# Cross attention and a two-expert feed-forward: an all-lane maximum at the start of GpSimd, expert chunks at step 10 in the shared tiles, column sums on GpSimd

## What is computed

```python
x = x + attention(layernorm(x), ctx, masks, Wq, Wk, Wv, Wo, bo)   # 16 heads of 64, 64 keys
z = layernorm(x)
top1 = argmax(softmax(z @ gate_w.T))                  # one of 2 experts
masked = z[None] * one_hot(top1).T[:, :, None]        # the expert that a row did not pick sees zeros
h = relu(einsum(masked, w1) + b1[:, None, :])
routing = (einsum(h, w2) + b2[:, None, :]).sum(axis=0)
shared = relu(z @ sw1 + sb1) @ sw2 + sb2
out = x + routing + shared
```

## Time and profile before

| what | value |
|---|---|
| median of 3 runs | 1909.89 us (1908.08 to 1910.09) |
| profiled execution, its own time | 1911.59 us |
| its span | 1909.8 us |
| TensorE busy | 1837.1 us, 96% |
| VectorE / ScalarE / GpSimd busy | 811.1 / 822.2 / 471.2 us |
| granted TensorE clock, mean | 0.984 |

### The profile page before, as it was taken

How to read it: one execution, slowest core, us unless ns; L and a number is a source line. 1 busy time by engine, 2 the same in 40 slices (tenths; PEclk the granted TensorE clock), 3 DMA queues, 4 the chain that set the end, 5 groups by cost and what they waited for, 6 DMA issues and landing times. The chain is left out here.

```text
span 1909.8 us, 33594 instructions
## 1 busy us (share of the span) xinstructions
PE 1837.1 (96%) x11584; PEld 1159.2 (61%) x11585; DVE 811.1 (42%) x1733; ACT 822.2 (43%) x1441; POOL 471.2 (25%) x443
## 2 busy tenths in 40 slices
PE   7979999999799999999999999999999999999997
PEld 5334445444456666666666666666666666666664
DVE  4977777777353444434333333222222222222222
ACT  3645555555333333334444444333333333433333
POOL 1036777777200000001000001121221112122111
PEclk9989999999899999999999999999999999999998
DMA  8225555555932232334433583822121111212100
GB/s 322 81 57 141 162 169 173 157 162 156 290 113 78 78 96 81 92 95 132 132 121 122 159 302 111 254 56 56 46 66 45 38 44 46 60 44 60 51 23 15
DMA packets 220647, 214.38 MB, mean 112 GB/s; under 512 B 121360, under 2 KB 162832, under 8 KB 220176
## 3 DMA queue, kind: packets, MB, share of 16 engines
q1 hardware_dynamic: 212640, 188.05, 33.1%
q0 software_dynamic: 7920, 25.17, 4.2%
HBM read 129.56 MB, written 58.98 MB: 99 GB/s over the span
## 5 line engine op out<-in xcount | busy, mean ns | idle before, releaser
L993 PE MATMUL pH<-room_a,room_w 128*128 128x256 f16 (+1 forms) x6336 | 768.9, 272 | 8.8 <-PEq L337 7.7
L1005 PE MATMUL pY<-room_w,room_a 128*128 128x512 f16 (+1 forms) x3120 | 755.3, 380 | 4.6 <-DVE room_a L1024 4.6
L993 PEld LDWEIGHTS pH<-room_a,room_w 128*128 (+1 forms) x6336 | 613.5, 98 | 188.7 <-issue 19.0
L1024 DVE TENSOR_TENSOR room_a<-room_a 128x256 f16<-128x256 f32 (+1 forms) x528 | 233.7, 443 | 915.0 <-ACT room_a L1018 914.9
L1005 PEld LDWEIGHTS pY<-room_w,room_a 128*128 128x128 f16 x3120 | 305.4, 98 | 268.2 <-DVE room_a L1024 4.8
L1016 ACT ACTIVATE room_a<-pH,e_bsel,sc 128x256 f32<-128x256 f32 (+1 forms) x272 | 152.1, 559 | 432.7 <-PE pH L993 407.8
L1016 ACT ACTIVATE room_a<-pH,b1s,sc 128x256 f32<-128x256 f32 x256 | 144.5, 564 | 385.8 <-PE pH L993 385.8
L1186 POOL TENSOR_TENSOR room_a<-room_a,s_brow 128x512 f32<-128x512 f32 x32 | 42.4, 1346 | 585.6 <-DVE room_a L1032 585.6
L467 PE MATMUL pO<-room_w,room_b 128*128 (+1 forms) x768 | 174.4, 384 | 4.8 <-DVE room_b L677 4.8
L1018 ACT ACTIVATE room_a<-pH,e_bsel,sc 128x256 f16<-128x256 f32 (+1 forms) x272 | 149.7, 550 | 0.0
L1018 ACT ACTIVATE room_a<-pH,b1s,sc 128x256 f16<-128x256 f32 x256 | 142.4, 556 | 0.0
(11 more groups left out here) (183 smaller groups left out, 1367.6 us busy)
## 6 DMA issues: line engine op xcount, KB each, us to landing
s_er<-in_w SPq DMA_DIRECT2D x64, 512.0 KB, 4.8
room_w<-e_split SPq DMA_DIRECT2D x8, 2048.0 KB, 18.3
rows_room<-in_x SPq DMA_DIRECT2D x32, 256.0 KB, 3.1
room_a<-in_sw SPq DMA_DIRECT2D x32, 256.0 KB, 4.2
room_b<-in_x SPq DMA_DIRECT2D x32, 256.0 KB, 3.9
s_split<-room_a SPq DMA_DIRECT2D x64, 128.0 KB, 3.8
x_scratch<-room_b SPq DMA_DIRECT2D x32, 256.0 KB, 4.1
z_split<-room_b SPq DMA_DIRECT2D x32, 256.0 KB, 4.1
```

Of the source, the lines that this page charges most:

```text
L993: mm = q.matmul(self.pH[j % 2][:, 0:rows], w[:, k, j * P:(j + 1) * P], zt[:, u, k, 0:rows], start=(n == 0), stop=(n == 3 * KC - 1))
L1005: mm = q.matmul(self.pY[u][r][:, :], h[:, j % self.HR, r * P:(r + 1) * P], w[:, j, :], start=(j == 0 and n == 0), stop=(j == HC - 1 and n ...
L1024: q.tensor_tensor(self.hl[:, j % self.HR, 0:rows], self.hf[:, j % self.HR, 0:rows], self.hh[:, j % self.HR, 0:rows], ALU.subtract).then_in ...
```

## The change

A maximum over the lanes of the constant column `half`, into a tile `warm` that nobody reads, stands behind the iotas in GpSimd's first block. `AT` goes from (8, 13) to (10, 13). The sums of `cacc` over the lanes are made by GpSimd, in place, in shared tile 9 (`PASS + 1`) behind the bias of tile 8; TensorE's two products and its wait for the idle rows are gone, and VectorE adds b2 to `cacc` itself.

```diff
+RADD = bass.bass_isa.ReduceOp.add
...
+                warm = sb("warm", [P, 1], F32, a)
...
                         pool.iota(starts[:, :], pattern=[[TOK, SLOT_TILES]], base=P, channel_multiplier=0, allow_small_or_imprecise_dtypes=True)
+                        pool.wait_ge(S["half_set"], 1)
+                        pool.partition_all_reduce(warm[:, :], half[:, :], P, RMAX)
                         pool.wait_ge(kv_done, 2 * PAIRS)
...
-        AT = (8, 13)
+        AT = (10, 13)
...
                         step(pool, g, u, -1, bias)
+                        if N * g + u == PASS + 1:
+                            pool.wait_ge(S["cacc"], 2 * TILES + 1)
+                            both = cacc[:, :, :].rearrange("p e n -> p (e n)")
+                            pool.partition_all_reduce(both, both, P, RADD).then_inc(S["cacc"], 1)
...
-                        if isinstance(g, int) and g == 0 and u == 1:
-                            pe.wait_ge(S["idle_row"], 2)
                         step(pe, g, u, 0, by_expert)
 
-                for e in range(2):
-
-                    pe.matmul(net.pY[1][e][:, :], ones[:, :], cacc[:, 1 - e, :], start=True, stop=True).then_inc(S["idle"], 1)
...
-                    dve.wait_ge(S["idle"], 2)
+                    dve.wait_ge(snet.S["cacc"], 2 * TILES + 2)
                     for e in range(2):
-                        dve.tensor_tensor(idle[:, e, :], net.pY[1][e][:, :], b2r[:, 0, :], ALU.add).then_inc(S["idle_row"], 1)
+                        dve.tensor_tensor(idle[:, e, :], cacc[:, 1 - e, :], b2r[:, 0, :], ALU.add).then_inc(S["idle_row"], 1)
```

More of the change, by code:

```diff
@@ L1433, in experts @@
         N, S, step, R = net.N, net.S, net.step, net.R
-        for n in ("b2_in", "flags", "idle", "idle_row", "pick_r", "pick_o", "bias", "sel0", "sel", "b2s", "bias0"):
+        for n in ("b2_in", "flags", "idle_row", "pick_r", "pick_o", "bias", "sel0", "sel", "b2s", "bias0"):
             S[n] = f.enter_context(nc.semaphore("e_" + n))
```

## The result

| | before | after |
|---|---|---|
| median (13 runs each) | 1909.8 us (1907.08 to 1913.42) | 1913.63 us (1912.12 to 1916.42) |
| ratio, 95% interval | | 1.0021 [1.0014, 1.0029] |
| profiled execution, its span | 1911.59 us, 1909.8 us | 1915.46 us, 1913.7 us |
| granted clock, mean | 0.984 | 0.985 |

The change makes the kernel 3.8 us slower; the forecast was 2.8 us, to 1912.7. Two effects of 8 and 13 us partly cancel, so the end alone proves little; the question is whether each is where the sum put it.

A forecast was written before the change was run, and what follows sets the result against it. TensorE, busy 96% of the span, was taken as the bound. On the profiled 1911.59 us, -8.3 + 12 - 0.9 = +2.8 gave 1914.4; with the timed median 1.7 us lower, the forecast was 1912.7 us, range 1900 to 1922.

The forecast's parts named there:

- Edit 1: Start: an early all-lane maximum on GpSimd takes the code load off the path and avoids TensorE's clock drop; -8.3 us.
- It just fits: Start: the `woT` transfer lands at 54.9 us, before VectorE's reduction would end at 55.6, so the 8.3 us stay.
- Rival C: Start: memsets displace the code and the load is paid again at `amr`; 1921.0 us, chance 0.05.
- Edit 2: Shared tiles 8 to 15: AT to (10, 13) makes ScalarE wait for the first chunk's stores; +12 us, 1.5 per tile.
- the free 3.3: Shared tiles: 3.3 us of ScalarE lateness costs TensorE nothing, read from tile 14 as 2.6 + 0.7; the rest is paid.
- Rival A: Shared tiles: the second chunk's lateness stays under 3.3 us, so AT's move is wholly hidden; 1900.7 us, chance 0.10.
- Edit 3: Column sums move from TensorE at the experts' start to GpSimd in shared tile 9, hidden there; -0.9 us.
- one more column added 15 to 30 ns: GpSimd all-reduce: price per column read from small ones, giving 0.35 + 15 to 31 us for 1024 columns; 25 taken.
- Free up to D = 48 us: Shared tile 9: GpSimd's sums cost nothing up to 48 us; beyond, each microsecond stops SyncE, then ScalarE, then TensorE.
- Rival B: Shared tile 9: at 129 ns a column the sums take 132 us, 84 beyond the free 48; 1997 us, chance 0.11.
- the experts' start: Without fp32 passes, the 36 first matmuls start at 1199.85 us, take 5.62 and end at 1205.47; -0.9 us.

The follow-up runs named there:

- the edit alone: The kernel before with only the early all-lane maximum on GpSimd added: 1901.59 us, ratio 0.9952.
- the run with an operation between: The changed kernel with AT back at (8, 13), plus one element-wise GpSimd addition between the early maximum and `amr`: 1921.85 us, ratio 1.0063.
- the run at (11, 13): The changed kernel with AT = (11, 13) in place of (10, 13): 1953.5 us, ratio 1.0228 to the kernel before.
- the kernel at (8, 13): The changed kernel with AT back at (8, 13), early maximum and GpSimd sums kept: 1902.28 us, ratio 0.9956 to the kernel before.
- the third edit alone: The kernel before with only the column sums moved to GpSimd, AT = (8, 13), no early maximum: 1910.55 us, ratio 0.9994.

## Why the prediction held, and where it was off

**Edit 1: right.** Forecast -8.3, the marks give -7.9 at attention and -8.4 at tile 7, the edit alone -0.48%. The parts are there: `amr` at 38.25 (38.6 forecast), no drop of the clock, a stand of 0.66 us (0.3 forecast). "It just fits" was wrong by half a microsecond: the `woT` transfer was issued 0.2 us later and took 12.4 us, not 11.9, so that VectorE waited for it, and of 8.7 us 8.1 were left. The last 0.5 us of the -8.4 came later and by chance: the stand ahead of the shared net was 6.68 us in place of 7.68 and the 36 matmuls behind it took 6.07 in place of 5.62, both of which vary from kernel to kernel by as much. The Trainium skill (GPSIMD Engine Reference, 2.1) gives about 6 us for a load that the first call pays. The trace agrees that no instruction shows it, but here it is paid at each change between kinds and not at a first call alone, and the gaps run from 5.85 to 9.39 us. Rival C is out, and the run with an operation between shows what it would have cost.

**Edit 2: right in its mechanism, 0.9 us low.** Forecast 7 x 1.5 + 1.6 = 12; measured 12.9, and the rows account for it: seven stands of 1.44 us on average (1.71 in tile 8), 1.35 us in tile 15, and 0.16 us for each of the eight, 12.7 together. ScalarE's lateness of 4.75 us in tiles 8 to 14 (4.8 forecast) less the free 3.3 leaves 1.45. The 3.3, which came from one tile of before, is what the prediction stood on. The runs bracket it: 2.1 to 2.3 us cost nothing, 3.6 cost 0.4, 4.75 cost 1.44. The first chunks of tiles 0 to 7, taken at nothing, cost nothing: from the bias of tile 1 to that of tile 7 a tile still takes 42.04 to 42.06 us. Rival A is out. The step that failed lies outside the change, in the expectation of the run at (11, 13): I computed the stand and not what the stand does to the clock, which is the same reckoning that I had made in edit 1.

**Edit 3: the net effect small, as forecast, but in part by luck.** The length of the all-reduce, D, was taken as 25 us and is 6.34: the step from "one more column added 15 to 30 ns" to a price per column failed. The two rows of two columns differ by 15 ns between themselves, 357 and 372, as much as the third column seemed to add; what I read as a price was scatter.

That it did no harm is luck. "Free up to D = 48 us" counted only GpSimd's own queue and left out VectorE, whose low halves are held up until 1.3 us before the all-reduce's end. In the kernel at (8, 13) one of them took 4.4 us more than usual and TensorE stood for 0.41 us, so about 4.0 us of such a delay are free. If VectorE is held up in the same way by a longer one, which no run here shows, an all-reduce of 25 us would have cost 17 to 19 us, my estimate from these rows (25 - 1.3 - 0.4 - 4.0, and up to 2.6 us less by where the low half falls). With the length that I took, my forecast of nothing would have been far off; the short length made it right.

Rival B stood on the same rows' upper bound, and on a figure of the Trainium skill for another instruction (GPSIMD Engine Reference, 3.2, 247.7 us over the partitions of [128, 2048]), from which 124 us was my estimate. The measured 6.34 us is a twentieth of that, so that figure should not be carried over to this instruction.

The other term is the experts' start, -0.4 in place of -0.9. The place was nearly right: the first product starts 1.8 us behind the end of the flags (1204.02 against 1202.26), 2.0 forecast (1199.85 against 1197.85). But its length was taken as 5.62 us from one execution of another start, and it is 6.37 here, and anywhere from 5.5 to 7.0 us from one kernel's execution to the next's, so that the term itself is known no better than that: in the profiled execution of the third edit alone they took 5.57 us, and the same two marks give -1.2. Behind the fp32 passes, which had kept TensorE at work, it was 4.5 to 5.2 us in three kernels. The Trainium skill (TensorE: Matmul & The Clock Gate, What's actually happening) says that the number of matmuls at the lower clock differs between runs of one kernel; the trace agrees, 5.52 and 6.83 us in two executions of the kernel at (8, 13). The removed work had been paying part of its own cost.

**The sum.** -8.4 + 12.9 - 0.4 = +4.1, against +2.8; the profiled executions differ by 3.9 and the medians by 3.8. The net errors of the three edits are -0.1, +0.9 and +0.5 us and do not hide each other. Inside edit 3 two errors did: too long an all-reduce, and no path from it to VectorE.

## What to carry to other kernels

An engine's wait costs what is queued behind it, less the time by which that was early: find the queued instruction, read its slack from a place in the trace where the lateness already occurs, and only then call a later step free. Work moved to an engine off the path can still hold up another engine beside it: before it is called free, look at what the neighbours' instructions take while it runs. Before an engine's work is taken away, see whether it holds up TensorE's clock for what follows; and a stand that is long enough to drop the clock is charged twice: here one of 3.95 us was, one of 1.7 us was not. A code load of GpSimd belongs into a wait that is there anyway, with nothing of the other kind between it and its use.

## What the hardware showed that I had not expected

- A lane sum of 1024 columns on GpSimd takes 6.1 to 6.4 us, 5.8 ns a column; of 32 columns 0.53 us.
- While it ran, a VectorE operation of 0.42 us took 2.5 to 4.8 us, and ended 1.3 us before the sum's end.
- The load at a change of kind took 5.85 to 6.59 us in the shared tiles and 6.62 to 9.39 us in the start. What sets its length was not found.
- Seven stands of about 1.5 us left the granted clock of TensorE at 1.00, one of 3.95 us brought a stretch of 0.79, and those of 10.3 us were followed by matmuls at 0.50. With work in the stand, and pauses of 0.65 and 1.07 us left at the experts' start and 2.19 us at the shared net's, the 36 took 4.22 and 4.09 us, as at the higher level.
